# Full attention on one core: the output projection of each 512-token chunk moved into the attention's last two units

## What is computed

```python
probs = jax.nn.softmax(jnp.einsum('bqhd,bkhd->bhqk', q, k), axis=-1)
att = jnp.einsum('bhqk,bkhd->bqhd', probs, v).reshape(b_, s_, h_)
x = x + att @ wo
xl2 = _ln(x, ln2_g, ln2_b)
...
```

## Time and profile before

| | |
|---|---|
| device time, median of 3 runs | 1312.14 us (1308.63 to 1313.78) |
| the profiled execution's own time | 1312.41 us |
| its span (first to last recorded work) | 1310.6 us |
| PE busy | 1140.5 us, 87% of the span |
| DVE busy | 884.6 us, 67% |
| ACT busy | 592.6 us, 45% |
| POOL busy | 425.6 us, 32% |
| first layer | last write of `att` ends at 157.04 us, last addition of `project_add` at 161.76 us |
| second layer | last write of `att` ends at 338.38 us, last addition of `project_add` at 343.10 us |

### The profile page before, as it was taken

The page is one execution under the profiler, slowest core; times in us unless marked ns, Lnnn a source line. Parts: engine busy times, 40 slices in busy tenths (PEclk is TensorE's granted clock), DMA queues, the critical chain, the costliest instruction groups (busy, mean ns, idle before and its releaser), DMA issues. The chain is left out here.

```text
span 1310.6 us, 29016 instructions
## 1 busy us (share of the span) xinstructions
PE 1140.5 (87%) x11396; PEld 689.9 (53%) x11396; DVE 884.6 (67%) x1510; ACT 592.6 (45%) x1392; POOL 425.6 (32%) x376
## 2 busy tenths in 40 slices
PE   6899899899898869999877999877995799974997
PEld 5577655577544448654446854534662454432343
DVE  3777545777456857534884733796665589999687
ACT  2566444666345659533657923402661355520100
POOL 0366401566206965312994530033441000000000
PEclk9899999899999979999997999998997889985999
DMA  3100000200002210011220000000000011100011
GB/s 79 61 15 2 2 13 17 75 2 1 2 1 57 56 29 3 2 67 32 57 52 2 4 15 13 12 4 4 5 5 1 13 22 21 19 6 1 13 31 45
DMA packets 52711, 28.05 MB, mean 21 GB/s; under 512 B 35458, under 2 KB 46188, under 8 KB 52204
## 3 DMA queue, kind: packets, MB, share of 16 engines
q1 hardware_dynamic: 52588, 26.33, 8.2%
HBM read 17.13 MB, written 1.05 MB: 14 GB/s over the span
## 5 line engine op out<-in xcount | busy, mean ns | idle before, releaser
L337 POOL TENSOR_TENSOR A_pr<-A_pr,A_rs 128x1024 f32<-128x1024 f32 x64 | 121.2, 1895 | 66.6 <-DVE A_rs L401 66.6
L391 DVE TENSOR_REDUCE A_mx<-psb 128x1 f32<-128x1024 f32 x64 | 77.8, 1215 | 21.2 <-PE psb L350 21.1
L434 ACT ACTIVATE A_pr<-psb,A_nm 128x1024 f32<-128x1024 f32 x64 | 71.5, 1117 | 22.9 <-DVE A_nm L395 22.6
L1164 POOL TENSOR_TENSOR F_raw<-F_raw,F_rc 128x1024 f32<-128x1024 f32 x32 | 75.6, 2363 | 17.3 <-DVE F_raw L1229 16.9
L361 PE MATMUL psb<-ident,A_pr 128*128 128x128 f32 x512 | 71.6, 284 | 3.1 <-POOL A_pr L337 3.1
L1881 ACT ACTIVATE M_hall<-psb,M_bu 128x512 f32<-128x512 f32 x64 | 44.0, 688 | 61.2 <-PE psb L1823 61.2
L361 PEld LDWEIGHTS psb<-ident,A_pr 128*128 128x128 f32 x512 | 56.2, 144 | 26.1 <-POOL A_pr L337 15.6
L2072 PE MATMUL psb<-M_hb,M_wd 128*128 128x512 f32 x128 | 68.2, 615 | 0.0
L1823 PE MATMUL psb<-XL,M_wu 128*128 128x512 f32 x128 | 66.8, 604 | 1.1 <-ACT M_ST L1890 1.1
L1194 PE MATMUL psb<-ident,F_raw 128*128 128x128 f32 x256 | 38.5, 298 | 33.3 <-POOL F_raw L1167 33.3
L1183 PE MATMUL psb<-F_wqkv,F_hst 128*128 128x512 f32 x128 | 61.6, 604 | 6.4 <-ACT F_hst L1241 4.5
(11 more groups left out here) (347 smaller groups left out, 2916.0 us busy)
## 6 DMA issues: line engine op xcount, KB each, us to landing
F_VS<-F_V SPq DMA_DIRECT2D x62, 128.0 KB, 2.3
F_raw<-in_c_xpos_dram SPq DMA_DIRECT2D x3, 1024.0 KB, 4.8
F_wqkv<-in_L_ffn_wqkv_dram SPq DMA_DIRECT2D x3, 768.0 KB, 7.2
A_w<-in_L_attn_w_dram SPq DMA_DIRECT2D x4, 256.0 KB, 3.3
M_wu<-in_L_ffn_Wup_dram SPq DMA_DIRECT2D x16, 64.0 KB, 2.0
M_wg<-in_L_ffn_Wgate_dram SPq DMA_DIRECT2D x16, 64.0 KB, 2.2
M_wd<-in_L_ffn_Wdown_dram SPq DMA_DIRECT2D x16, 64.0 KB, 1.8
M_sel<-in_c_select_dram SPq DMA_DIRECT2D x16, 64.0 KB, 1.9
```

The source lines that it names most:

```text
L337: pool.tensor_tensor(p, p, rs[:, u % 2:u % 2 + 1].broadcast_to([P, SEQ]), ALU.mult).then_inc(scaled, 1)
L391: dve.tensor_reduce(mx[:, u % 2:u % 2 + 1], sview(u), AX, ALU.max).then_inc(maxed, 1)
L434: act.activation(pr[:, u % NP, :], sview(u), ACT.Exp, bias=nm[:, u % 2:u % 2 + 1], scale=scale, accum_out=su[:, u % 2:u % 2 + 1]).then_inc ...
L1164: pool.tensor_tensor(rs[:, o, :], rs[:, o, :], rc[:, o, :], ALU.add).then_inc(unit, 1)
```

## The change

The block `project_add` is gone. `full_attention` gets the matrix and the destination, and two functions of its own: `project(c)` on PE, one product of `wo` with chunk c of `att` into `bank[c]`, and `add(c)` on DVE. The four products are issued at fixed places: `project(0)` in step 31 ahead of `turn(30)`, `project(1)` in step 32 ahead of `turn(31)`, `project(2)` behind `turn(31)`, `project(3)` behind `mix(15)`. Each waits until the exponential has read the scores in its bank and until the four tiles of its chunk are written. DVE adds chunks 0 and 1 ahead of `put(15)` and chunks 2 and 3 behind it.

```diff
-        def project_add(tag, weights, sources, dst):
...
-        def full_attention(tag, QH, QL, KH, KL, V, scale, result, bias, loads):
+        def full_attention(tag, QH, QL, KH, KL, V, scale, result, bias, loads, weight, dst):
...
+                        def project(c):
+                            pe.wait_ge(exped, NU - 1 + c // 2)
+                            pe.wait_ge(put_out, 4 * c + 4)
+                            pe.matmul(bank[c], weight, result[:, cs(c)], start=True, stop=True, skip_group_check=True).then_inc(summed, 1)
+
                         scores(0)
                         scores(1)
                         for u in range(NU + 1):
                             if u + 2 < NU:
                                 scores(u + 2)
+                            if u >= NU - 1:
+                                project(u - NU + 1)
                             if u:
                                 turn(u - 1)
                             if u >= 3 and u % 2:
                                 mix(u // 2 - 1)
+                        project(2)
                         mix(NT - 1)
+                        project(3)
...
+                        def add(c):
+                            dve.wait_ge(summed, c + 1)
+                            dve.tensor_tensor(dst[:, cs(c)], dst[:, cs(c)], bank[c], ALU.add).then_inc(added, 1)
...
+                        add(0)
+                        add(1)
                         put(NT - 1)
+                        add(2)
+                        add(3)
...
-                    project_add("A3", [wo[:]], [att], H)
+                                   wo[:], H)
```

More of the change, by code:

```diff
@@ L309, in full_attention @@
             NP = 4
-            g = (scored, maxed, negated, exped, inverted, scaled, turned, kept_a, kept_v, mixed, put_out, loaded) = sems(
-                "full", "scored maxed negated exped inverted scaled turned kept_a kept_v mixed put_out loaded")
+            g = (scored, maxed, negated, exped, inverted, scaled, turned, kept_a, kept_v, mixed, put_out, loaded, summed, added) = sems(
+                "full", "scored maxed negated exped inverted scaled turned kept_a kept_v mixed put_out loaded summed added")
             with ExitStack() as st:
@@ L1044, in build @@
                                    lambda sp, sem: issue(sp, sem, table_parts(0) + window_weights(0) + [
-                                       (mask[:].bitcast(U16), a["c_window"].rearrange("p (v n) -> p v n", v=2))]))
-                    project_add("A3", [wo[:]], [att], H)
+                                       (mask[:].bitcast(U16), a["c_window"].rearrange("p (v n) -> p v n", v=2))]),
+                                   wo[:], H)
                 g = loaded, hid_rdy, sloped, sig_rdy, hid_out, sum_rdy, added, tabled = sems("A4", "loaded hid_rdy sloped sig_rdy hid_out sum_rdy added tabled", st)
```

## The result

The changed kernel takes 1308.14 us, the median of 20 runs (1303.71 to 1317.91); the kernel before, in 20 runs beside them, 1314.03 us (1308.63 to 1321.94). The ratio is 0.9959 with a 95% interval of 0.9946 to 0.9972, which is 5.4 us less, between 3.7 and 7.1. The profiled execution's span is 1307.4 us against 1310.6.

What follows compares the result with a forecast made beforehand. Nothing of project_add is hidden, and PE is the bound between its two holes ahead of it. Per layer -0.32 + 0.10 - 3 x 0.86 + 0.94 = -1.86 us; two layers: 1312.14 - 3.7 = 1308.4 us, range 1304.5 to 1313.0.

Steps and rivals of the forecast that it cites:

- The removed 5.00 us: From the last write of att to the next block's first work, in each layer: the time the change removes, 5.00 us.
- `project(0)` at no cost: Ahead of turn(30): PE's 1.54 us hole covers the product, cost 0, with 0.6 us left; 0.94 without that cover.
- `project(1)` on the path at 0.94: Ahead of turn(31), where there is no hole: the product pushes everything behind it back by 0.94 us, at least 0.86.
- `project(2)` at no cost: Between turn(31) and mix(15): the product fits the 0.83 us hole, cost taken as 0, bounds 0 and 0.11 us.
- `add(0)` and `add(1)` at no cost: On DVE ahead of put(15): both additions end before put(15) is released, cost 0, with 0.7 us to spare.
- The end: Behind the last write: semaphore 0.10 us, project(3) to its addition 1.13, addition ending 159.90, barrier 0.28, next block at 160.18.
- D: Distance from turn(30)'s start to next table load; as rival, project(0) and project(2) cost 0.94 us each, 1312.1 us, chance 0.10.
- The clock term, set to 0 in the middle: PE's clock behind the change: slow stretches of about 1.7 us added or saved, 0 in the middle, +-2 stretches in the range.
- path: Theory in the follow-up runs: the gain is the shortened stretch, 1.84 us a layer, and the total follows it.
- A: Rival: the clock falls at the attention's new end, 1.7 us per layer where it happens, 1311.8 us with both; chance 0.12.
- B: Rival: slower, as waits behind the changed layers are newly punished by the clock; three added stretches give 1313.5 us; chance 0.05.
- C: Rival: project(1) costs nothing because turn(31) has slack, gain 5.6 us, 1306.5 us; chance 0.13.

Runs made afterwards that it cites:

- the warm start: Three idle 512-column products added in the opening block: on the kernel before 1309.68 us, ratio 0.997; on the changed kernel 1303.18 us, ratio 0.9911.
- the kernel without chunk 1: Changed kernel without the product and addition of chunk 1, leaving that chunk of H without the attention's output: 1305.7 us, ratio 0.9934.
- the best version: Changed kernel with project(1) moved behind project(0) ahead of turn(30) and the last product split into 384 and 128 columns: 1303.3 us, ratio 0.9922.
- four products at the end: Changed kernel with all four products and additions behind the last write, still in the attention's block: 1314.61 us, ratio 1.0006.

## Why the prediction was right

The forecast was 1308.4 us against a measured 1308.14, and 3.7 us of gain against 5.4 (3.7 to 7.1). The agreement of the two totals to 0.3 us is partly luck: the median of before was 1312.14 in its first three runs and 1314.03 in 20, and this 1.9 us hides the 1.7 us by which the gain was forecast too small.

- *The removed 5.00 us:* right, with both barriers. The barrier that stays takes 157.64 - 157.36 = 0.28 us.
- *`project(0)` at no cost:* right. The hole left is 0.68 us, forecast 0.6.
- *`project(1)` on the path at 0.94:* right. By the timeline it is 0.96 us from its start to `turn(31)`, by its removal 0.91. As forecast, it is the one product whose place was chosen badly.
- *`project(2)` at no cost:* right. `mix(15)` starts 1.87 us after `turn(31)`, before 1.92; DVE's copy (152.24 + 0.69 = 152.93) releases it 0.10 us later, as it did before; the product, at its price of 0.94, is done at 152.98, which is as near a tie as the forecast had it.
- *`add(0)` and `add(1)` at no cost:* right. They end at 154.13, `put(15)` starts at 155.04; 0.9 us to spare, forecast 0.7.
- *The end:* the write's semaphore takes 0.15 us to PE, forecast 0.10; the 1.13 us to the addition came exactly. D = 10.36 against 10.34 on paper.
- *The clock term, set to 0 in the middle:* whether it was right is open. I took added and saved slow stretches to be equally likely, 1.7 us each. The gain's interval, 3.7 to 7.1 us, just reaches the forecast; but all eight sets with products inside the attention came out under their path, by 1.0 to 4.1 us, while the traces, good to some 3 us, show no rest. The price of 1.7 us each holds for `n2` alone: inside the attention's first 90 us a clock time lost of 1.71 us in the changed kernel and of 3.41 in the same kernel with the warm start stand beside 89.01 and 89.35 us.

Of the rivals, A (the clock falls at the new end of the block) didn't come: the clock is 1.00 over both stretches. The rule of the Trainium skill's page "Perfetto Trace Analysis", "Matmul Optimizations", that batches of matmuls should run back to back, would have made it A; here the batch of four was split and the clock stayed at 1.00 over it; the sets of runs lost less clock time, not more, and those of `before` with one more batch of four lost 8.8 us more. B's mechanism came in the second layer's `n2` of both traces of the changed kernel, once each, but in one of two traces of the kernel before as well. C fell with the kernel without chunk 1. D fell with the first hole: two products fit into it.

## What to carry to other kernels

A small block between two large ones is paid in full, since nothing runs beside it: of 5.00 us here the extra barrier was 0.23, and 1.6 us more (3.1 in the best version) came back only when products were put into holes of the engine that sets the pace. Put each piece into a hole that the timeline shows, and look at the pieces that got none; the one in front of `turn(31)` cost its full 0.91 us, and moved into the hole two rows earlier 0.02. What waits for the last result should be as small as that result: 128 of 512 columns gave 0.57 us a layer.

A term of 4 us in 1310 can be checked to 0.02 us in the timeline and not to better than 2 us in the total. Read it in the stretch. Before you put the total's rest down to the clock, see in the traces whether the loss lies behind the first changed instruction: here it lay ahead of it.

## What the runs showed of the hardware

- The same wait of PE in `n2`, 1.48 or 1.49 us, was followed by a clock of 0.50 in one layer and of 1.00 in the other in one trace of the kernel before, and by the fall in both layers in its other trace and in the changed kernel: such a wait doesn't fix the level by itself.
- What a stretch at the lower clock costs depends on where it falls. In `n2` one cost 1.66 us (42.58 against 40.92). In the first layer's attention, 90 us long with the clock at 0.50 from 56.9 to 67.1, against 56.4 to 59.8, the longer one cost 1.23 us for some 3 us more of clock time lost.
- The opening can run at the lower level, by its durations: in the trace with four products at the end, the first norm's block took 20.70 us instead of 12.38, with the MATMUL pair of L171 there at 2.05 us instead of 1.10. The clock column of that stretch says 1.00 all the same, because the trace's records of the clock begin only at 30.9 us there (at 5.1 to 16.8 us in the others), so that the durations have to tell it:

```profile
12.60:33.30 20.70, 19.66 (x72) 15.33 (x72) 5.91 (x10) 4.41 (x8) 0.00 (x0) 1.00 0.18 45
```

- Three products without use at the start, while the input is on its way, made the whole program 3.9 us faster (2.0 to 5.9). Some 1.1 us of it lies in the transposes of the input; where the rest comes from no run shows.
